# Pixel sums of two tiles taken together on TensorE in a fused group norm, channel norm and 1x1 convolution

## What is computed

```python
def reference(x, L0_conv_W, L0_conv_b):
    def _L0_conv_ref(x, W, b):
        EPS = 1e-06
        u = jnp.mean(x, axis=1, keepdims=True)
        var = jnp.var(x, axis=1, keepdims=True, ddof=1)
        s = jnp.sqrt(var)
        n_x = (x - u) / (s + EPS)
        n_x = jnp.einsum('bchw,oc->bohw', n_x, W) + b[None, :, None, None]
        return x * n_x
    def _gn(v, G=32, eps=1e-5):
        ...
        return ((g - m) / jnp.sqrt(s + eps)).reshape(v.shape)
    x = x + _L0_conv_ref(_gn(x), L0_conv_W, L0_conv_b)
    return x
```

## Time and profile before

| quantity | value |
|---|---|
| median of 3 runs | 1963.65 us (1959.81 to 1964.78) |
| the profiled execution | 1956.86 us |
| its span, first to last instruction | 1955.1 us |
| PE busy | 1738.8 us, 89% |
| DVE busy | 1797.6 us, 92% |
| ACT busy | 1438.8 us, 74% |
| POOL busy | 1453.9 us, 74% |
| mean granted TensorE clock | 0.992 of full speed |
| HBM traffic | 341 GB/s over the span |

### The profile page before, as it was taken

One profiled execution on the slowest core, in us unless ns is written; L12 is line 12 of the kernel. 1 busy time (PEld: TensorE's weight loads), 2 busy tenths in 40 slices (PEclk: granted clock), 3 DMA queues, 4 the chain that ended last, 5 costly groups with the idle time before them and its releaser, 6 DMA issues.

```text
span 1955.1 us, 55325 instructions
## 1 busy us (share of the span) xinstructions
PE 1738.8 (89%) x22562; PEld 986.7 (50%) x22562; DVE 1797.6 (92%) x2120; ACT 1438.8 (74%) x2498; POOL 1453.9 (74%) x1684
## 2 busy tenths in 40 slices
PE   0079998999899998999989999899988999899998
PEld 0055554555455554555545555555545555455554
DVE  5669999999899998999989999999989999998887
ACT  5598885888768885788858888588866888544442
POOL 0077877878778886788768787787877888788885
PEclk9989999999999999999999999999999999999999
DMA  9989998999999998999989999899998999844775
GB/s 379 390 311 341 375 377 305 398 374 375 333 313 403 359 387 322 336 392 371 384 307 384 375 379 356 308 409 374 374 333 321 391 362 385 321 192 188 268 253 221
DMA packets 184140, 670.84 MB, mean 343 GB/s; under 512 B 20688, under 2 KB 21072, under 8 KB 183888
## 3 DMA queue, kind: packets, MB, share of 16 engines
q1 hardware_dynamic: 110160, 398.85, 55.3%
q10 hardware_dynamic: 73728, 268.47, 34.6%
HBM read 398.80 MB, written 268.44 MB: 341 GB/s over the span
## 4 chain that ended last, share of the span: by engine, by line
PE 48%; DVE 27%; issue 9%; DMA 9%; POOL 2%; ACT 2%; SPq 2%; POOLq 0%; ACTq 0%; DVEq 0%
PE proj_ps L733 27%; PE sums_ps L722 12%; DVE scaled L632 9%; PE factor_ps L708 9%; DMA tiles<-x 6%; DVE tiles L645 5%; DVE bn L676 4%; DVE bn L677 4%; DMA out<-tiles 3%; SPq L408 2%; POOL tiles L441 1%; DVE var L651 1%; POOL tiles L452 1%; ACT unused L509 1%; DVE gn L580 1%
## 5 line engine op out<-in xcount | busy, mean ns | idle before, releaser
L733 PE MATMUL proj_ps<-scaled,w_t 128*128 128x512 f32 x2048 | 997.5, 610 | 0.2 <-DVE scaled L632 0.2
L452 POOL TENSOR_SCALAR tiles<-tiles,out_shift 128x1024 f32<-128x1024 f32 x512 | 573.9, 1121 | 233.8 <-DVE tiles L645 218.9
L645 DVE SCALAR_TENSOR_TENSOR tiles<-proj_ps,gate_shift,tiles 128x1024 f32<-128x1024 f32 x512 | 642.8, 1255 | 46.7 <-PE proj_ps L733 46.3
L441 POOL TENSOR_SCALAR tiles<-tiles,norm_scalars 128x1024 f32<-128x1024 f32 x512 | 615.8, 1203 | 58.0 <-DMA tiles<-x 57.0
L509 ACT ACTIVATE unused<-tiles,bn 128x1024 uint8<-128x1024 f32 x560 | 634.9, 1134 | 2.0 <-issue 1.7
L632 DVE TENSOR_TENSOR scaled<-tiles,factor_ps 128x1024 f32<-128x1024 f32 x512 | 618.1, 1207 | 8.7 <-PE factor_ps L708 8.0
L524 ACT ACTIVATE squares<-tiles 128x1024 f32<-128x1024 f32 x512 | 537.5, 1050 | 100.5 <-POOL tiles L441 71.9
L733 PEld LDWEIGHTS proj_ps<-scaled,w_t 128*128 128x128 f32 x2048 | 351.9, 192 | 248.5 <-issue 247.5
L708 PE MATMUL factor_ps<-pieces,pick_sb 128*128 128x128 bf16 x4096 | 319.7, 221 | 104.3 <-DVE scaled L632 89.8
L722 PEld LDWEIGHTS sums_ps<-tiles,const_sb 128*32 128x32 f32 x8192 | 193.7, 109 | 397.9 <-issue 263.6
L722 PE MATMUL sums_ps<-tiles,const_sb 128*32 128x128 f32 x8192 | 332.0, 280 | 12.2 <-ACT squares L524 12.2
(11 more groups left out here) (56 smaller groups left out, 672.5 us busy)
## 6 DMA issues: line engine op xcount, KB each, us to landing
tiles<-x SPq DMA_DIRECT2D x760, 512.0 KB, 9.4
out<-tiles ACTq DMA_DIRECT2D x512, 512.0 KB, 6.7
const_sb<-const SPq DMA_DIRECT2D x1, 193.5 KB, 2.3
scaled<-w SPq DMA_DIRECT2D x1, 64.0 KB, 2.1
scaled<-ident SPq DMA_DIRECT2D x1, 64.0 KB, 2.1
pick_sb<-pick SPq DMA_DIRECT2D x1, 8.0 KB, 2.2
bias_sb<-bias SPq DMA_DIRECT2D x1, 0.5 KB, 2.2
```

What stands on the lines that cost most here:

```text
L441: nc.gpsimd.tensor_scalar(place(s), place(s), norm_scalars[:, 0:1], norm_scalars[:, 1:2], ALU.add, ALU.mult).then_inc(normed, 1)
L452: nc.gpsimd.tensor_scalar(place(s), place(s), 1.0, out_shift[:, 0:1], ALU.mult, ALU.add).then_inc(finished, 1)
L645: nc.vector.scalar_tensor_tensor(out=place(s), in0=proj_ps[:, s % 2, :], scalar=gate_shift[:, 0:1], in1=place(s), op0=ALU.add, op1=ALU.mul ...
L733: mm = nc.tensor.matmul(proj_ps[:, s % 2, h:h + BANK], w_t[:, :], scaled[:, s % 2, h:h + BANK], start=True, stop=True)
```

## The change

PE takes no sums in an even step. In an odd step it takes the sums of the previous tile and of its own tile in one go, and does so before the step's spread and project instead of behind them. ACT gets a wait before sum_sq: sum_sq shares its memory with the factor that POOL reads, and PE's order no longer implies that POOL is done with it.

```diff
                     if (done := set_behind(step, LAG_VAR, b, own, before)) is not None:
                         statistics(b + 1, step, of, SUM_SQ_AFTER)
+                        if done > 1:
+                            act.wait_ge(pieces_done, done - 1)
                         act.wait_ge(summed, b * slots + step)
@@
+                    if own and step % 2:
+                        sums(b, step - 1, before)
+                        sums(b, step, before)
                     if (s := behind(step, LAG_SPREAD, own, before)) is not None:
                         spread(b, step, s)
                     if (s := behind(step, LAG_FACTOR, own, before)) is not None:
                         project(b, step, s)
-                    if own:
-                        sums(b, step, before)
```

## The result

The changed kernel takes 1972.51 us (median of 6 runs, 1971.25 to 1974.68) against 1962.23 us of the kernel before in 6 runs: ratio 1.0056, interval 1.0046 to 1.0067. It is slower by half a per cent, as forecast in sign; the forecast time of 1980 us was 7.5 us too high. The profiled execution took 1974.68 us, its span is 1972.9 us, 17.8 us more than the span before.

What follows compares the result with a forecast made beforehand. The kernel was taken to alternate between a DVE bound and a PE bound. Sets adding +13.9 us in 7 images and +2.4 in the last, changes of images even, gave 1963.65 + 16.3 = 1980 us, range 1946 to 1998 us.

Steps and rivals of the forecast that it cites:

- What bounds the kernel: Sets of four steps alternate between a DVE bound (14.23 us) and a PE bound (13.35 us); PE bounds the last image.
- Double sets: Sets with statistics of two tiles on DVE, 9 an image: 14.23 us to 13.98, or 14.52 with two passes in step 2.
- The two new prices on PE: 0.43 us between the sums of two tiles, 1.78 us from project straight to spread; 0.42 us less PE work a set.
- The ring: Closed chain gate(0), scale(1), scale(2), spread(2), proj(2), two tiles' sums, spread(3), proj(3), gate(0): other sets take 13.50 us, loss 0.15.
- The wait for squares: Odd tile's sums wait for ACT's squares(3) where step 2 has two statistics passes: 14.52 us, in 5 of 16 sets.
- the single set with two passes: Set with one tile's statistics on DVE and two passes in step 2, one an image: 14.52 against 13.35, loss 1.17.
- The sum: Gains and losses of all sets: +1.98 us per image with statistics, +13.9 for 7 images, +2.4 in the last.
- The changes of images: Longer gap and clock falls against earlier sums at each change of images: counted as even, between -2 and +11 us in all.
- Only PE counts: Rival: DVE's distances give way, other sets reach 12.93 us and double sets 13.98; 1921 us, chance 0.13.
- Cancel: Rival: squares(3) isn't late, double sets all gain 0.25 us and the others lose 0.15; 1958 us, chance 0.22.
- More clock falls: Rival: gaps at changes of images and after late loads bring seven to ten further clock falls, +11 to +16 us; 1992 us, chance 0.13.

Runs made afterwards that it cites:

- e5: Kernel before with only sums(0) and sums(1) taken together, ahead of spread(1), and no new ACT wait: 1943.36 us, ratio 0.9902.
- e6: Kernel before with sums(0) moved ahead of spread(0), directly behind sums(3), the rest as before: 1947.93 us, ratio 0.9934.
- e7: Changed kernel, step 2's second statistics pass behind squares(3), ACT's sum_sq ahead of the statistics pass, DVE's L651 and its successor ahead of gate(0): 1931.85 us, ratio 0.9852.
- e4: Kernel before with only sums(2) and sums(3) taken together, ahead of spread(3), keeping ACT's new wait: 1990.31 us, ratio 1.0148.
- e2: Changed kernel with step 2's second statistics pass moved behind squares(3) on ACT: 1958.69 us, ratio 0.9991 to the kernel before.
- e1: Kernel before with only ACT's new wait for pieces ahead of sum_sq: 1961.35 us, ratio 1.001.
- e3: Kernel before with step 2's second statistics pass moved behind squares(3) on ACT: 1960.29 us, ratio 1.0.
- e10: Changed kernel with step 2's second statistics pass behind squares(3) and ACT's sum_sq ahead of the statistics pass, DVE's order kept: 1957.84 us, ratio 0.9985.
- e8: Kernel before, no pair of sums, with DVE's L651 ahead of gate(0) and ACT's sum_sq ahead of the statistics pass: 1983.57 us, ratio 1.0114.
- e9: Kernel before with sums(0) and sums(1) together ahead of spread(1), DVE's L651 ahead of gate(0) and ACT's sum_sq earlier: 1979.51 us, ratio 1.0094.

## Why the prediction was right, and where it was off

**What bounds the kernel**: right. Double sets are DVE's and the others PE's. With less work on PE the sets of the last image fell from 13.35 to 13.10 us (e5, e6); double sets stayed at 14.23 in e6 and fell to 13.88 when DVE's operations were shortened (e7).

**The two new prices on PE**: right. Sums of two tiles in a row start 0.43 us apart (1810.52 to 1810.95), 0.46 where the odd tile's squares are only just ready (1817.60 to 1818.06), and project to spread is 1.77 us (1819.53 to 1821.30). For the earlier trace rows the profile gives a granted clock of 1.00; that PE ran at half clock there was read from the times alone, and the 0.43 bears it out. That PE gains is shown by e5 and e6: 13.10 us a set with one pair, 13.14 forecast. Here the rule of the Trainium skill on draining at a change of tiling mode ("TensorEngine Tiling (Array Packing)", section "Tiling Modes") agrees with the trace: fewer changes, less time on PE. Whether it is the draining that costs, or another difference between the two kinds of matmul, no run here separates.

**The ring**: right, 13.54 us measured for 13.50, the difference being 0.46 instead of 0.43 between the two tiles' sums in the pair ahead of spread(3), and 2.50 instead of 2.49 from gate(0) to scale(1). The 0.46 is squares(3) again: it starts at 1816.94, and the odd sums 1.12 us behind it. The prediction had called squares(3) just in time, 7.59 against 7.57. It argued the ring from starts and distances; e4 (longer, 13.74), e5 (only one tile in it) and e7 (shortened on DVE) show the ring. The double sets without a late squares(3), 13.98, came out to the hundredth.

**The wait for squares**: right in place and size, 14.51 us for 14.52, and shown by e2. One term was too small: the single set with two passes was put at 14.52 us and takes 14.83. In that set the first tile of the image passes gate. DVE does a small copy before it, and the rows show scale(2) at T + 3.33 instead of 3.10:

```profile
1059.41 1.21 DVE L634 TENSOR_TENSOR scaled<-tiles,factor_ps 128x1024 f32<-128x1024 f32 x1
...
1061.40 0.09 DVE L644 COPY gate_shift<-new_scalars 128x1 f32<-128x1 f32 x1
...
1062.74 1.21 DVE L634 TENSOR_TENSOR scaled<-tiles,factor_ps 128x1024 f32<-128x1024 f32 x1
...
1064.29 0.40 ACT L533 ACTIVATE piece<-sum_sq,const_sb 128x128 bf16<-128x128 f32 x1 [1.74 <-DVE sum_sq L669]
```

The piece copy follows at T + 4.88, where it was T + 4.58, and squares(3) starts at T + 7.78 and not 7.48. The first set of the last image, which has no statistics at all, shows the same: scale(2) at T + 3.33, and 13.85 us where the other sets take 13.54. This is read from the rows and was not tried.

**The sum**: 13 sets were to lose 1.5 us and lost 1.97 (0.3 by that set, the rest by the ring's 0.04 in three). The spans of the two profiled executions differ by 17.8 us, and 16.3 were forecast: 5.6 up to the second image, where about 2 were counted, 6 x 1.97 = 11.8 in the next six, -3.7 in their changes, +4.2 in the last image, where 2.4 were counted. The changes of images were called even, between -2 and +11 us in all. The -3.7 lies outside, but one execution can't tell it from even: over the same six changes e1 and e3, which have no pair, differ from the profiled execution of before by -0.7 and +2.8 us, and e4, e10 and e2 by -1.2, 0.0 and +3.0. Longer were those of e5 and e6, +6.0 and +5.9 us, and of e8 and e9, +10.0 and +12.3; why was not looked for.

**The time, where it was off.** 1963.65 + 16.3 = 1980 us was 7.5 us too high. Of this 1.4 us are the starting point: over six runs the median of before is 1962.23 us. The other 6.0 us are the difference, 16.3 forecast and 10.3 between the medians. The oversized term can't be one of the repeating sets, which lost more than was forecast, not less (1.97 us for 1.5 in 13 sets; the last image lost 4.2 for 2.4). So it lies in the rest, above all the changes of images: they were put at nothing and must have come out below that. Single ones took between 47 and 52 us in each of the two profiled executions. The 17.8 us between the two spans don't confirm the 16.3 either: the execution of before was faster than all six of its runs, and that of the changed kernel was the slowest of its six. What of the 17.8 us is not in the medians was not settled. That the time came within 0.4% is thus in part luck: some terms were too small and one was too large.

**The rivals.** "Only PE counts" (1921 us) was wrong as long as the ring stood; e7, 1931.85 us, comes nearest to it, with double sets of 13.88 and sets of 13.00 us in the last image for 12.93. "Cancel" (1958 us) is close to what e2 measured, 1958.69, once squares(3) was in time. More clock falls: the mean granted clock is 0.990 to 0.994 in the six runs of the changed kernel, within the 0.988 to 0.996 of the kernel before in the runs beside e1, and the changes of images, where the falls were expected, took no longer; so there is no sign of this case.

## What to carry to other kernels

When two engines feed each other through single buffers, draw the ring and add up its members before moving work on one of them: work moved ahead of a hand-over lengthens the ring even if the engine has less to do in all. The same saving can be had at another place of the schedule; here the pair ahead of spread(1) or spread(0) gave 0.7 to 1.0%, and the pair ahead of spread(3) cost 1.5%. And look for what an edit makes possible rather than for its own gain: the pair ahead of spread(3) only paid when DVE's order was changed to use its early sums, 1931.85 us.

## What the runs showed of the hardware

Two things had not been expected. Small DVE operations of 0.23 and 0.31 us took 1.07 and 0.81 us where they met POOL's tensor operations, and ended about 0.1 us behind them; moved away from one, DVE lost the time at the next (L657 from 1.07 to 0.23 us, L669 from 0.31 to 0.81).

The other is that PE lost time to a late operand without a gap in its own records. The sums over the odd tile of the pair ahead of spread(3) start 0.46 us behind the sums before them in the changed kernel and 0.55 in e7, with the same instructions that take 0.43 in the other pair. Each time they start 1.12 us behind the start of squares(3), as in the earlier trace rows, where it was 1.11. The first row is from the last image of the changed kernel (the matmul that follows is the one of 1818.06 above), the others are from e7; PEld is PE's loading of weights. In e7 it alone has the wait on record, in the changed kernel no row has it:

```profile
1816.94 1.06 ACT L524 ACTIVATE squares<-tiles 128x1024 f32<-128x1024 f32 x1
```

```profile
1808.32 1.07 ACT L524 ACTIVATE squares<-tiles 128x1024 f32<-128x1024 f32 x1
...
1808.89 0.62 PE L724 MATMUL sums_ps<-squares,const_sb 128*32 128x128 f32 x16
1809.44 0.38 PEld L724 LDWEIGHTS sums_ps<-tiles,const_sb 128*32 128x32 f32 x16 [0.20 <-ACT squares L524]
1809.44 0.65 PE L724 MATMUL sums_ps<-tiles,const_sb 128*32 128x128 f32 x16
```

So about 0.12 of the 13.00 us in e7 are still a wait for squares(3), and PE's own work would be 12.88, beside the 12.93 forecast. This is an estimate from these rows, and no run tried it.
